# Retention: queries, keys and state in 16-bit parts, and the rows' centring on ScalarE

## The reference

```
q = x @ q_w + q_b;  k = (x @ k_w + k_b) * 16 ** -0.5
v = x @ v_w + v_b;  g = x @ g_w + g_b
qr = q * cos + rotate_every_two(q) * sin        # kr in the same way
qk = einsum('bhmd,bhnd->bhmn', qr, kr) * mask   # lower triangle, decay per head
qk = qk / clip(abs(qk.sum(-1)), 1)
out = einsum('bhmn,bhnd->bhmd', qk, v)
out = (out - mean(out)) / sqrt(var(out) + 1e-5)
return (silu(g) * out) @ o_w + o_b
```

## Time and profile before

| | us |
|---|---|
| median of 3 runs (1024.1 to 1029.89) | 1029.05 |
| the profiled execution | 1025.94 |
| its span | 1024.1 |
| TensorE busy in the span | 874.4 (85%) |
| VectorE busy | 784.2 (77%) |
| ScalarE busy | 615.7 (60%) |
| GpSimd busy | 372.5 (36%) |

### The profile page before, as it was taken

How to read it: one execution, slowest core, us unless ns; L and a number is a source line. 1 busy time by engine, 2 the same in 40 slices (tenths; PEclk the granted TensorE clock), 3 DMA queues, 4 the chain that set the end, 5 groups by cost and what they waited for, 6 DMA issues and landing times. The chain is left out here.

```text
span 1024.1 us, 22180 instructions
## 1 busy us (share of the span) xinstructions
PE 874.4 (85%) x8762; PEld 579.5 (57%) x8762; DVE 784.2 (77%) x1460; ACT 615.7 (60%) x1108; POOL 372.5 (36%) x326
## 2 busy tenths in 40 slices
PE   1386878788488899999689999998799998999997
PEld 0122323232246555565356777776689975778786
DVE  8899989833788899887678899887577886667443
ACT  5578789887476554452155555554578865656431
POOL 1043435321247140000246667666144641224220
PEclk9998889898679899999899999999799999999999
DMA  5403232320420030000120000000200000000000
GB/s 148 83 1 48 36 54 32 48 37 1 135 72 1 2 135 1 1 2 1 58 111 1 3 2 2 2 3 2 73 2 2 2 1 1 2 12 11 12 22 31
DMA packets 21670, 30.47 MB, mean 30 GB/s; under 512 B 6000, under 2 KB 17982, under 8 KB 20416
## 3 DMA queue, kind: packets, MB, share of 16 engines
q1 hardware_dynamic: 18816, 26.44, 11.2%
q10 hardware_dynamic: 2752, 2.62, 0.9%
HBM read 18.56 MB, written 2.10 MB: 20 GB/s over the span
## 5 line engine op out<-in xcount | busy, mean ns | idle before, releaser
L589 ACT ACTIVATE t_pT<-t_sc 128x1536 f32<-128x1536 f32 x96 | 136.7, 1454 | 28.8 <-PE t_sc L696 28.5
L269 POOL TENSOR_SCALAR_AFFINE_SELECT t_pT<-t_pT 128x512 f32<-128x512 f32 x64 | 75.9, 1206 | 167.4 <-ACT t_pT L589 167.3
L696 PE MATMUL t_sc<-t_qk 32*128 32x512 f16 (+3 forms) x1152 | 89.1, 365 | 47.4 <-DMA t_qk<-t_sin_parts 26.6
L696 PEld LDWEIGHTS t_sc<-t_qk 32*128 32x128 f16 x1152 | 37.1, 99 | 107.0 <-issue 50.4
L2686 POOL TENSOR_SCALAR_AFFINE_SELECT r_att<-r_att 128x1024 f16<-128x1024 f16 x64 | 69.5, 1108 | 66.2 <-DVE r_att L2726 66.2
L717 PE MATMUL t_ot<-t_pT,t_v 128*17 128x512 f32 (+3 forms) x768 | 81.3, 535 | 11.3 <-DVE t_ou L433 5.1
L1983 PE MATMUL c_pso<-ck_VO,c_pT 128*128 128x256 f16 x480 | 55.0, 273 | 1.4 <-DVE c_pT L1824 1.4
L2726 DVE TENSOR_TENSOR r_att<-r_pss,r_att 128x1024 f16<-128x1024 f32 x32 | 39.1, 1221 | 20.2 <-ACT r_att L2852 20.2
L1983 PEld LDWEIGHTS c_pso<-ck_VO,c_pT 128*128 128x128 f16 x480 | 46.3, 98 | 6.7 <-DVE c_pT L1824 1.6
L2268 ACT ACTIVATE m_sg<-m_psg 128x512 f32<-128x512 f32 x32 | 19.1, 596 | 51.6 <-PE m_psg L2311 51.5
L2852 ACT CAST r_att<-r_pss 128x1024 f16<-128x1024 f32 x32 | 32.4, 1012 | 28.0 <-PE r_pss L2922 28.0
(11 more groups left out here) (593 smaller groups left out, 2408.7 us busy)
## 6 DMA issues: line engine op xcount, KB each, us to landing
t_qk<-t_cos_parts SPq DMA_DIRECT2D x24, 128.0 KB, 5.4
t_qk<-t_sin_parts SPq DMA_DIRECT2D x24, 128.0 KB, 7.0
x<-in_x ACTq DMA_DIRECT2D x4, 512.0 KB, 7.3
out_x<-x SPq DMA_DIRECT2D x8, 256.0 KB, 2.1
r_rcos<-in_ret_cos SPq DMA_DIRECT2D x1, 1280.0 KB, 9.1
r_rsin<-in_ret_sin SPq DMA_DIRECT2D x1, 1280.0 KB, 10.6
t_qk<-t_cos_parts SPq DMA_DIRECT2D x16, 64.0 KB, 2.7
gw_raw<-in_gateT SPq DMA_DIRECT2D x1, 1024.0 KB, 7.6
```

The lines of the kernel that those rows point to most:

```text
L269: last = g.affine_select(out=blk, in_=blk, compare_op=ALU.is_ge, fill=0.0, base=0, pattern=[[0, 4], [1, P]], channel_multiplier=-1)
L589: a.activation(pT[:, at:at + 3, :].rearrange("p a s -> p (a s)"), sc[s % 2][:], ACT.Exp, scale=CURVE * CURVE / math.sqrt(2 * DH)).then_inc ...
L696: last = t.matmul(sc[s % 2][:, 512 * k + at:512 * k + at + w], qk[r, g % 3, 1, of_k, P * i:P * i + P], qk[r, g % 3, 0, of_q, q0:q0 + w], s ...
```

## The change

The rotated queries and keys, the keys' values and the state become f16 parts, and their products f16 products. The rotated sum stays in PSUM (`psq`); ScalarE copies it as f16 (`rotated_high`), VectorE subtracts (`rotated_low`), so each head's 32 columns hold 16 high and 16 low parts. GpSimd writes a second copy of the keys with the parts exchanged (`swap`), so that two products give high and low by high and low. `delta` makes four products a head in place of one, `weigh` two with the state's parts. The state's split into two f16 parts is made on GpSimd (`split_state`), and its layout as `u` moves from GpSimd to ScalarE, four products a tile with a column of 0 and 1 as the scale, at the end of ScalarE's step. The f32 copy of the values (`v32`, L2868) is gone; `values_low` reads PSUM and multiplies by 1/GAIN itself, and what waited for `v_done` waits for `vlo_done`. The centring of x's rows moves from VectorE to ScalarE, with an offset prepared by `offsets`.

```diff
+    def offsets(self, v, n):
+        t = slice(*self.SPANS[n])
+        v.wait_ge(self.rs_ready, n + 1)
+        v.scalar_tensor_tensor(self.sm[:, 0, t], self.sm[:, 1, t], -1.0, self.sm[:, 3, t], ALU.mult, ALU.mult).then_inc(self.nm_ready, 1)
+    def center_on_scalar(self, a, t):
+        a.wait_ge(self.nm_ready, sum(t >= b for b, _ in self.SPANS[1:]))
+        wait(a, self.turned, t - 1)
+        a.activation(self.xn[:, t % 2, 0:D - 1], self.x[:, t, 0:D - 1], ACT.Identity, bias=self.sm[:, 0, t:t + 1],
+                     scale=self.sm[:, 3, t:t + 1]).then_inc(self.normed, 1)
...
-            def expand(t):
+            def split_state(t):
                 if inside(t) and t % TB != TB - 1:
                     g.wait_ge(kept_state, t + 1)
-                    wait(g, pv_done, t)
-                    g.tensor_tensor(u[:, (t + 1) % 2], us[:, t % 2].unsqueeze(2).broadcast_to((P, 4, 4, VC)),
-                                    rowtile[:].unsqueeze(1).unsqueeze(3).broadcast_to((P, 4, 4, VC)), ALU.mult).then_inc(u_done, 1)
+                    wait(g, u_done, t)
+                    own.link(g.tensor_copy(us16[:, t % 2, 0], us[:, t % 2]))
+                    g.tensor_tensor(us16[:, t % 2, 1], us[:, t % 2], us16[:, t % 2, 0], ALU.subtract).then_inc(us_split, 1)
                 elif inside(t):
                     g.wait_ge(kept_state, t + 1)
-                    g.tensor_copy(tiny[:], us[:, t % 2, 0, 0:1]).then_inc(u_done, 1)
+                    g.tensor_copy(tiny[:], us[:, t % 2, 0, 0:1]).then_inc(us_split, 1)
+            def swap(t):
+                if inside(t):
+                    keys, swap_ = rot[:, t % ROTS, 1], rot[:, t % ROTS, 2]
+                    g.wait_ge(rot_low, t + 1)
+                    g.tensor_copy(swap_[:, :, 0:KD], keys[:, :, KD:2 * KD])
+                    g.tensor_copy(swap_[:, :, KD:2 * KD], keys[:, :, 0:KD]).then_inc(swapped, 1)
...
                 power(s - 1)
-                expand(s)
+                swap(s + 2)
+                split_state(s)
...
-                    v.wait_ge(v_done, t + 1)
-                    v.tensor_tensor(v16[:, q, 1, :, 0:VD], v32[:, q, :, 0:VD], v16[:, q, 0, :, 0:VD], ALU.subtract).then_inc(vlo_done, 1)
+                    v.scalar_tensor_tensor(v16[:, q, 1, :, 0:VD], psv[:].rearrange("p (h d) -> p h d", h=HR), 1.0 / GAIN,
+                                           v16[:, q, 0, :, 0:VD], ALU.mult, ALU.subtract).then_inc(vlo_done, 1)
...
+                    v.tensor_tensor(psq[:], psq[:], rb[:], ALU.add).then_inc(rot_done, 1)
+            def rotated_low(t):
+                if inside(t):
+                    parts = rot[:, t % ROTS, 0:2]
+                    v.wait_ge(rot_high, t + 1)
+                    v.tensor_tensor(parts[:, :, :, KD:2 * KD], psq[:].rearrange("p (a h d) -> p a h d", a=2, h=HR),
+                                    parts[:, :, :, 0:KD], ALU.subtract).then_inc(rot_low, 1)
...
                 low(s, 0)
-                x_center(s + 5)
...
                 low(s, 1)
+                rotated_low(s + 2)
                 centre(s - 1)
+                values_low(s + 1)
                 state(s)
                 add(s - 3)
                 z_low(s - 2)
-                values_low(s + 1)
...
+            def rotated_high(t):
+                if inside(t):
+                    wait(a, k_turned, t - ROTS + 1)
+                    wait(a, d_ready, t - ROTS + 1)
+                    a.wait_ge(rot_done, t + 1)
+                    a.copy(rot[:, t % ROTS, 0:2, :, 0:KD], psq[:].rearrange("p (a h d) -> p a h d", a=2, h=HR)).then_inc(rot_high, 1)
+            def expand(t):
+                if inside(t):
+                    a.wait_ge(us_split, t + 1)
+                    wait(a, pv_done, t)
+                    if t == 0:
+                        a.wait_ge(s_c, 3)
+                    for h in range(4):
+                        last = a.activation(u[:, (t + 1) % 2, :, :, h, :], us16[:, t % 2], ACT.Copy, scale=rowtile[:, h:h + 1])
+                    last.then_inc(u_done, 1)
...
                 high(s, 1)
+                rotated_high(s + 2)
...
                 silu(s - 1)
+                x_center(s + 5)
+                expand(s)
...
             def gates(t):
                 if inside(t):
-                    upto(t_, v_done, t + 3)
+                    upto(t_, vlo_done, t + 3)
```

More of the change, by code:

```diff
@@ L2677, in _ @@
                 own.link(g.memset(rowtile[32 * h:32 * h + 32, h:h + 1], 1.0))
+            own.link(g.memset(id16[:], 0.0))
+            g.affine_select(out=id16[:], in_=id16[:], compare_op=ALU.not_equal, fill=1.0, base=0,
+                            pattern=[[-1, P]], channel_multiplier=1).then_inc(s_c, 1)
+            g.memset(v16[:, :, 0, :, VD:VC], 1.0).then_inc(s_c, 1)
+            g.memset(v16[:, :, 1, :, VD:VC], 0.0).then_inc(s_c, 1)
             ahead.power(g, 2)
@@ L2796, in state @@
                         new = us[:, t % 2]
-                    wait(v, u_done, t - 1)
+                    wait(v, us_split, t - 1)
                     v.tensor_tensor(us[:, t % 2], new, keep[:].unsqueeze(2).broadcast_to((P, 4, VC)), ALU.mult).then_inc(kept_state, 1)
@@ L2813, in _ @@
                 low(s, 0)
-                x_center(s + 5)
+                if s == STEPS[0]:
+                    ahead.offsets(v, 1)
+                if s == STEPS[0] + 3:
+                    ahead.offsets(v, 2)
                 gate(s - 2)
@@ L2858, in copy_turned @@
                         wait(a, pv_done, t - 1)
-                    a.copy(qkT[:, t % 2, n].rearrange("p g m -> p (g m)"), ptr[:]).then_inc(done, 1)
+                    which, wide = (slice(0, 1), 512) if n == 0 else (slice(1, 3), 1024)
+                    a.copy(qkT[:, t % 2, which].rearrange("p a g m -> p (a g m)"), ptr16[:, 0:wide]).then_inc(done, 1)
+            def rotated_high(t):
[13 more added lines that the diff above has]
+                    last.then_inc(u_done, 1)
             def values(t):
@@ L2883, in x_high, with x_center @@
                     ahead.high(a, t, psq)
+            def x_center(t):
+                if inside(t) and t >= FIRST:
+                    ahead.center_on_scalar(a, t)
             for s in STEPS:
@@ L2921, in score @@
                             r = slice(32 * h, 32 * h + 32)
-                            last = mm(pss[:, j, P * g:P * g + P], qkT[r, q, 1, g, :], qkT[r, q, 0, g, :], start=(g == 0), stop=True, skip_group_check=True)
+                            mm(pss[:, j, P * g:P * g + P], qkT[r, q, 1, g, :], qkT[r, q, 0, g, :], start=(g == 0), stop=False, skip_group_check=True)
+                        for j in range(2):
+                            h = 2 * half + j
+                            r = slice(32 * h, 32 * h + 32)
+                            last = mm(pss[:, j, P * g:P * g + P], qkT[r, q, 2, g, :], qkT[r, q, 0, g, :], start=False, stop=True, skip_group_check=True)
                     last.then_inc(scored, 1)
@@ L2936, in weigh @@
                         if t % TB:
-                            mm(pso[:, bank, c0:c0 + 4 * VC], qkT[:, q, 0, g, :], u[:, q, g].rearrange("p h d -> p (h d)"),
-                               start=(g % 2 == 0), stop=False, skip_group_check=True)
+                            for part in range(2):
+                                mm(pso[:, bank, c0:c0 + 4 * VC], qkT[:, q, 0, g, :], u[:, q, part, g].rearrange("p h d -> p (h d)"),
+                                   start=(g % 2 == 0 and part == 0), stop=False, skip_group_check=True)
                         for h in range(4):
@@ L2961, in values @@
                     wait(t_, z_ready, t - 2)
-                    wait(t_, v_done, t)
+                    wait(t_, vlo_done, t)
                     project(t, psv[:], 512, v_psum)
@@ L2994, in turn_qk @@
                         t_.wait_ge(q_copied, t + 1)
-                    for g in range(4):
-                        last = t_.transpose(ptr[:, P * g:P * g + P], rot[:, t % ROTS, n, 4 * g:4 * g + 4, :].rearrange("p h d -> p (h d)"), ahead.ident[:])
+                        t_.wait_ge(swapped, t + 1)
+                    for which in (0,) if n == 0 else (1, 2):
+                        for g in range(4):
+                            to = P * (4 * (which // 2) + g)
+                            last = t_.transpose(ptr16[:, to:to + P], rot[:, t % ROTS, which, 4 * g:4 * g + 4, :].rearrange("p h d -> p (h d)"), id16[:])
                     last.then_inc(done, 1)
@@ L3016, in delta @@
                     q = t % 2
-                    t_.wait_ge(v_done, t + 1)
-                    t_.wait_ge(rot_done, t + 1)
+                    t_.wait_ge(vlo_done, t + 1)
+                    t_.wait_ge(swapped, t + 1)
                     wait(t_, kept_state, t)
                     for g in range(4):
-                        for h in range(4):
-                            last = mm(psd[32 * h:32 * h + 32, VC * g:VC * g + VC], rot[:, t % ROTS, 1, 4 * g + h, :], v32[:, q, 4 * g + h, :],
```

(7 more changed lines are left out.)

39 lines of the change are left out of this document (14 added, 25 removed).

## The result

| | us |
|---|---|
| before, median of 4 runs beside it | 1028.01 |
| after, median of 4 runs (1085.07 to 1091.78) | 1089.48 |
| ratio after to before, 95% interval | 1.0598 [1.0551, 1.0645] |
| forecast | 1079 (1060 to 1099) |
| the profiled execution after, and its span | 1088.66, 1086.9 |

A forecast was written before the change was run, and what follows sets the result against it. TensorE's order was taken to bound the old step (12.32 us), a closed loop of waits the new (15.6). 39.4 - 0.4 + 5.7 + 2.5 + 1.5 + 3.3 = +52.0 gave 1077.9 or 1081; forecast 1079 us (1060 to 1099).

The forecast's parts named there:

- The circle over the four engines: Retention stage: masks, power, swap, split, products, next high and low form a closed loop of waits, 15.6 us a step.
- six links: The loop's stretches from low(s,0) round to the next step's low, claimed to sum to 15.6 us (14.2 to 16.6).
- the products: ScalarE's four expand products at the end of its step, claimed at 1.92 us, from below 1.05.
- TensorE's saving: TensorE's step in the retention stage falls by about 1.0 us, with none of it in the loop's 15.6 us.
- `low(s,1)` to `power`: Stretch from VectorE's low(s,1) to GpSimd's power, second mask between: 3.53 us, at worst 0.6 more.
- the start: Stage's start: rotated_high and rotated_low in series before the second projection may overwrite the bank, +1.5 us.
- the end: Stage's end: squares(15) stands behind expand(15) and two normalisations, coming at about 711.0 instead of 707.67, +3.3 us.
- The clock: Rival: TensorE's gaps keep it at the lower clock, a step grows to 17.9 us, total 1109 us; chance 0.08.
- the second lap: Rival: rotate, copies, transposes, values, gates, silu, centring, expand and high set the step, 14.6 us, total 1066; chance 0.12.
- first lap: The loop of waits through GpSimd's split and ScalarE's products sets the step at 15.6 us; chance 0.75.
- TensorE's work: TensorE's time per step in the retention stage falls by about 1.0 us, between +0.1 and -1.7, to some 11.3.

The follow-up runs named there:

- the kernel of 11.98 us a step: Changed kernel with ScalarE's query copy ahead of expand(s - 1), x_center ahead of silu, GpSimd's power last, VectorE's order rotated_low, state, values_low, centre: 1022.1 us.

## Why the prediction was right, and what it missed

**Right: the sign, the mechanism, the period's cause.** The circle over the four engines was read from the diff and five groups of rows, and of its six links four came within 0.1 us and the products within 0.28. The circle was opened as a whole (39 us), and two links were taken out singly: `swap` (0.68 a step at the full clock) and `power` (down to the next bound). That the kernel before was bound by TensorE is shown by the kernel without the state product. That TensorE's saving is worth nothing in the changed kernel follows from the rows, without a run of its own: a `score` half takes 0.55 us instead of 1.09, a group of `weigh` 0.42 instead of 0.62, TensorE is busy for 116.86 of 160 us in the stage's middle where it was for 158.38, and a step in which its values took 1.3 us longer was no longer than the others (16.10).

**Missed, the largest: `low(s,1)` to `power`.** The text said that `rotated_low` "doesn't lengthen it as long as the centred variance is there when the mask ends; at worst it adds 0.6". The condition wasn't met. In before `centre` ended as the mask did, with nothing to spare, and `rotated_low` pushed it back by its 0.6; it also pushed L2782 into the mask, where it waits for a selection to end (0.68 instead of 0.18). Together, less what the shorter L2783 and L2787 give back, that is 0.93 a step, an estimated 12 us in 13 laps. The kernel with `centre` first shows the 0.93 in its short steps; over its 12 steps 8.3 us came back, since in the others the lower clock takes part of it.

**Mis-sized: the products**, 1.64 in place of 1.92: the nearest row was of two f32 instructions with scale and bias from tiles; these four f16 ones follow each other at 0.41. Over 13 laps that gave 3.6 us back and hid part of the other miss.

**Mis-sized: the start**, 5.3 in place of 1.5. I counted two operations in series and overlooked what stands behind them: the query copy behind `rotated_high(1)`, and the lower clock that the wait brings for 2.8 us of TensorE. The query copy is worth 3.4 us by experiment (19.8 to 16.5); the 1.9 us that are left are near the 1.5 of the sum.

**Mis-sized: the end**, 0.8 in place of 3.3. Two things are in it. `squares(15)` came 2.5 us later against step 15's mask, not 3.3 (10.92 us behind it, 770.57 - 759.65, where it had been 707.67 - 699.22 = 8.45). And the last output product, which ran at the lower clock in before, ran at the full one in after, which gives 1.3 us back. Before, then after:

```profile
716.36 2.74 PE L2982 MATMUL r_psd<-ra_wo,r_zT 128*128 128x256 f16 x12 [1.41 <-DVE r_zT L2809]
```

```profile
778.97 1.48 PE L3040 MATMUL r_psd<-ra_wo,r_zT 128*128 128x256 f16 x12 [1.40 <-DVE r_zT L2833]
```

**The clock** was a rival with 17.9 us a step. It did fall, for a part of some steps: the values take 2.77 instead of 1.46 at 607.34, behind a wait of 1.75 (and 1.46 a step later, behind one of 2.27). But the second lap had 1.23 us to spare, and in such a step ScalarE reaches the products just as the split ends:

```profile
606.51 1.03 PE L3057 MATMUL r_ptr<-r_id,r_rot 128*128 128x128 f16 x8 [1.75 <-ACT r_qkT L2888]
607.34 2.77 PE L3006 MATMUL r_psv<-ra_w,ra_xT 128*128 128x512 f16 x6
...
614.03 1.74 ACT L2905 ACTIVATE r_u<-r_us,r_rowtile 128x264 f16<-128x264 f16 x4
```

The steps stay 16.10 us. It was right to leave it out of the sum, though for a narrower reason than the one I gave, that the gaps are shorter. In the kernels with a shorter first lap the same fall does lengthen steps: 14.43 against 13.15, 15.57 against 15.17.

**Not bearing on the result:** TensorE's work fell by 1.9 us a step, not 1.0 (score -1.08, weigh -0.8, transposes -0.24, `delta` +0.2), more than my bounds allowed; the terms as written also add up to -0.1 at the upper end, not +0.1. The text also said that GpSimd would be the engine with the least idle time; it is busy for 11.41 of 20 us, less than VectorE and TensorE. A lap that goes round over four engines fills none of them, and the place to look is the brackets, not the busy shares. The 1.4 us ahead of the stage and 1.5 behind it lie within what these stretches scatter by from trace to trace.

## What to carry to other kernels

Before an operation is moved to the end of another engine's step, follow its new wait to its source, and from the first instruction behind it forward: if that path reaches the source again, the sum of the links is a period, whatever the engines' shares. Such an operation is best done one step late, where the data has long been there: the same instructions then cost 39 us less. When a queue gets a new operation, ask of each one behind it who waits for it, and keep small VectorE operations with two SBUF inputs out of the time of GpSimd's long ones.

## What the runs showed of the hardware

VectorE's small operations on two SBUF inputs wait while a mask of GpSimd runs: L2783 (128x16) took 1.06 or 1.00 beside one and 0.17 without in the kernel of 11.98 us a step, L2822 (128x132) 1.08 and 0.28, L2782 0.68 and 0.17, and they end as a selection (1.07 us) ends. `rotated_low`, 0.68 beside the same mask, has one input in PSUM and loses nothing: behind the mask, in the kernel with `centre` first, it takes 0.68 too (603.29). The Trainium skill (SBUF — State Buffer, Who interferes with whom) says that a VectorE instruction with two SBUF inputs contends with a GpSimd instruction that reads SBUF, as one of its inputs comes over a shared port; the trace agrees, and adds that at these sizes the price is the rest of GpSimd's instruction, up to six times the operation's own length.

Sixteen f16 products of 32 rows, 128 columns, alternating between two row groups, started within 0.55 us (617.97 to 618.52), 0.034 each, where transposes over all rows take 0.055. The 64 products of `delta` (32 columns of the array, 33 moving) started within 0.59 us (624.46 to 625.05), 0.009 each.
